# An LSTM and a GRU over one sequence on one core: the input weights are split by tick 1, and the LSTM's third step stands ahead of the condition's products and of the GRU's first step

## The reference

```
x (32, 128, 512), cond (32, 512)
# 1: LSTM over 128 steps, h0 = cond, c0 = 0
a  = x_t @ Wx + b + h @ Wh           # 2048 columns: i, f, o, g
c  = sigmoid(f)*c + sigmoid(i)*tanh(g);   h = sigmoid(o)*tanh(c)
x  = x + hs                          # y in the kernel
# 2: GRU over 128 steps of y, h0 = 0, with a condition
z  = sigmoid(y_t @ W_z + h @ U_z + cond @ C_z + b_z)
r  = sigmoid(y_t @ W_r + h @ U_r + cond @ C_r + b_r)
hh = tanh(y_t @ W + (r*h) @ U + cond @ C + b)
h  = (1-z)*h + z*hh
return y + hs
```

## Time and profile before

| | us |
|---|---|
| median of three executions | 1199.74 |
| the profiled execution's own time | 1200.66 |
| its span, first to last instruction | 1198.9 |
| TensorE busy | 1176.5 (98%) |
| VectorE busy | 981.0 (82%) |
| ScalarE busy | 464.0 (39%) |
| GpSimd busy | 334.0 (28%) |
| mean granted TensorE clock | 0.997 |

### The profile page before, as it was taken

How to read it: one execution, slowest core, us unless ns; L and a number is a source line. 1 busy time by engine, 2 the same in 40 slices (tenths; PEclk the granted TensorE clock), 3 DMA queues, 4 the chain that set the end, 5 groups by cost and what they waited for, 6 DMA issues and landing times.

```text
span 1198.9 us, 75562 instructions
## 1 busy us (share of the span) xinstructions
PE 1176.5 (98%) x34514; PEld 863.3 (72%) x34514; DVE 981.0 (82%) x2906; ACT 464.0 (39%) x1117; POOL 334.0 (28%) x614
## 2 busy tenths in 40 slices
PE   7899999999999999999999999999999999999997
PEld 2477676666667777777787777877777777777775
DVE  3869777888878888888888888888888888888876
ACT  5664334344333333333333333333333333333332
POOL 0100233333222223233232232322223323223221
PEclk9999999999999999999999999999999999999999
DMA  9701401111011111011111001111101111101001
GB/s 377 259 4 22 154 11 21 21 21 21 5 21 21 22 22 21 6 22 22 22 22 22 13 13 22 22 22 22 18 9 22 22 22 22 22 7 19 13 13 21
DMA packets 138272, 43.73 MB, mean 36 GB/s; under 512 B 131504, under 2 KB 131520, under 8 KB 136416
## 3 DMA queue, kind: packets, MB, share of 16 engines
q1 hardware_dynamic: 137632, 38.55, 13.2%
q10 hardware_dynamic: 192, 0.33, 0.1%
q0 software_dynamic: 128, 0.01, 0.0%
HBM read 30.49 MB, written 8.39 MB: 32 GB/s over the span
## 4 chain that ended last, share of the span: by engine, by line
PE 96%; DVE 2%; DMA 1%; issue 1%; ACT 0%; POOL 0%; SPq 0%; DVEq 0%; POOLq 0%
PE ps_g L996 40%; PE ps_l L996 34%; PE ps_l L1059 15%; PE ps_g L1005 3%; PE ps_c L1059 2%; PE ps_l L1005 2%; DMA stage<-in_L_cond_b_dram 1%; DMA wh<-in_L_cond_Wx_dram 1%; DVE wh L671 0%; DVE zr L674 0%; DVE rg L916 0%; ACT zr L584 0%; DVE rgT L918 0%; DVE wx L671 0%; DVE rg2T L668 0%
## 5 line engine op out<-in xcount | busy, mean ns | idle before, releaser
L996 PE MATMUL ps_l<-wh,h2T 128*32 128x512 f16 x5952 | 345.1, 380 | 0.3 <-issue 0.3
L996 PE MATMUL ps_g<-w,y2T 128*32 128x384 f16 x5760 | 256.3, 326 | 0.0
L996 PEld LDWEIGHTS ps_l<-wh,h2T 128*32 128x32 f16 x5952 | 157.1, 97 | 132.8 <-issue 1.9
L996 PEld LDWEIGHTS ps_g<-w,y2T 128*32 128x32 f16 x5760 | 159.3, 97 | 87.6
L429 POOL TENSOR_TENSOR yT<-xT,hT 128x128 f32<-128x128 f32 x128 | 61.9, 483 | 531.0 <-DVE hT L853 531.0
L996 PE MATMUL ps_g<-u,g2T 128*32 128x256 f16 x5760 | 179.5, 273 | 0.0
L996 PEld LDWEIGHTS ps_g<-u,g2T 128*32 128x32 f16 x5760 | 156.2, 97 | 14.6
L674 DVE SCALAR_TENSOR_TENSOR zr<-ps_g,sc,term 128x256 f32<-128x256 f32 x128 | 61.8, 483 | 76.9 <-PE ps_g L996 74.6
L382 POOL TENSOR_TENSOR o_area<-yT,gT 128x128 f32<-128x128 f32 x127 | 58.2, 458 | 192.2 <-DVE gT L977 191.4
L996 PE MATMUL ps_g<-u,rg2T 128*32 128x128 f16 x5760 | 102.7, 219 | 3.1 <-DVE rg2T L668 2.9
L612 ACT ACTIVATE g2T<-gT,sc 128x128 f16<-128x128 f32 x120 | 48.3, 402 | 131.6 <-DVE gT L977 131.6
(11 more groups left out here) (140 smaller groups left out, 1799.2 us busy)
## 6 DMA issues: line engine op xcount, KB each, us to landing
out_dram<-o_area SPq DMA_DIRECT2D x124, 64.0 KB, 1.9
x_nat<-in_x_dram SPq DMA_DIRECT2D x120, 64.0 KB, 2.7
wh<-in_L_cond_Wx_dram SPq DMA_DIRECT2D x4, 1024.0 KB, 8.8
stage<-in_L_cond_Wx_dram SPq DMA_DIRECT2D x4, 1024.0 KB, 9.9
w<-in_L_cond_Wh_dram SPq DMA_DIRECT2D x3, 1024.0 KB, 15.6
u<-in_L_cond_Wh_dram SPq DMA_DIRECT2D x1, 1024.0 KB, 21.0
stage<-in_L_cond_W_z_dram SPq DMA_DIRECT2D x1, 1024.0 KB, 23.2
stage<-in_L_cond_W_r_dram SPq DMA_DIRECT2D x1, 1024.0 KB, 25.5
```

Of the source, the lines that this page charges most:

```text
L996: mm = nc.tensor.matmul(bank[B * j:B * j + B, c0:c1].rearrange("p (n c) -> p n c", c=B), still(a, k), moving(b, k, j), start=opens and (a, ...
```

## The change

The GRU's biases get a slab of their own and are loaded at the start, and spread at chunk 3 of `wx`. The input's products of step 2 go from the loop over `wx` into tick 0, between the chunks of h0 with `wh`, and those of step 3 stand half there and half behind. All of `wx` is split by the end of tick 0: on ScalarE `wx_high(3)` before tick 0, on VectorE `wx_low(2)` before it and `wx_low(3)` behind its state. The LSTM's step 2 (`T_AHEAD`) moves on every engine from tick 2 into tick 1: on TensorE behind y(0) with W and ahead of the condition's products, on VectorE into the row of `wh_low`, ahead of the condition's sum and of the GRU's step 0. All four `wh_high` stand ahead of it on ScalarE.

```diff
+        T_AHEAD = T_WH + 1
-        biases = stage[0:1, GG + 2, :]
+        l_biases, g_biases = stage[0:1, GG + 1, :], stage[0:1, GG + 2, 0:GG * D]
@@ gpsimd
-            pool.wait_ge(spread_ps, 1)
             for g, b in enumerate((b_z, b_r, b_h)):
...
@@ scalar
             wx_high(2)
+            wx_high(3)
             wh_squared(1)
...
                 if t == T_WH:
-                    wx_high(3)
...
                     wh_high(2)
+                    wh_high(3)
...
             def after_cand(t):
-                if t == T_WH:
-                    wh_high(3)
...
-                if runs_lstm(t):
...
+                if runs_lstm(t) and t != T_AHEAD:
+                    lstm_step(t)
...
                 if t == T_WH:
                     after_state(t)
+                    lstm_step(T_AHEAD)
@@ vector, before tick 0
+            dve.wait_ge(spread_ps, 2)
+            nc.vector.tensor_copy(term1[:], ps_g[0][:, 0:GG * P]).then_inc(term_done, 1)
+            dve.wait_ge(term_done, 2)
...
             wx_low(1)
-            dve.wait_ge(spread_ps, 2)
-            nc.vector.tensor_copy(term1[:], ps_g[0][:, 0:GG * P]).then_inc(term_done, 1)
-            dve.wait_ge(term_done, 2)
+            dve.wait_ge(wx_hi, 2)
+            wx_low(2)
@@ vector, after_state
                 if t == 0:
-                    dve.wait_ge(wx_hi, 2)
-                    wx_low(2)
+                    dve.wait_ge(wx_hi, 3)
+                    wx_low(3)
                 if t == T_WH:
                     common(0, 0)
                     lstm_scales(1, 1)
-                    dve.wait_ge(wx_hi, 3)
-                    wx_low(3)
-
-                    wh_low(0, 0)
-                    wh_low(0, 1)
-                    wh_low(1, 0)
+                    for k in range(K - 2):
+                        for half in range(HALVES):
+                            wh_low(k, half)
+                    new_sums(T_AHEAD, T_AHEAD, 0)
+                    wh_low(2, 0)
+                    new_cell(T_AHEAD)
+                    wh_low(2, 1)
+                    new_state(T_AHEAD, T_AHEAD)
 
                     dve.wait_ge(cond_ps, 1)
...
             def after_keep(t):
                 if t == T_WH + 1:
-                    wh_low(2, 1)
+                    wh_low(3, 0)
...
             def after_cand(t):
-                if t == T_WH:
-                    wh_low(1, 1)
-                    wh_low(2, 0)
                 if t == T_WH + 1:
-                    wh_low(3, 0)
                     wh_low(3, 1)
@@ tensor
+                if k == 3:
+                    pe.wait_ge(bias1_in, 16 * GG)
+                    spread(ps_g[0], g_biases, GG * P)
+                input_as_given(0, k)
+                input_as_given(1, k)
...
+            def recurrent_as_given(t):
+                pe.wait_ge(hT_done if t > 0 else h0T_done, max(t, 1))
+                state = hT[:, (t - 1) % 2, :] if t > 0 else h0T[:]
+                for k in range(K):
+                    if t == 0:
+                        pe.wait_ge(wh_in[k], 16)
+                    done = as_given(ps_l[t], 0, state, wh_raw[k], k, False, k == K - 1)
+                    if t == 0 and k < 2:
+
+                        input_as_given(2, 2 * k)
+                        input_as_given(2, 2 * k + 1)
+                    if t == 0 and k == 2:
+                        input_as_given(3, 0)
+                        input_as_given(3, 1)
+                done.then_inc(gates_ps, 1)
+                if t == 0:
+                    input_as_given(3, 2)
+                    input_as_given(3, 3)
...
-                if t == 1:
+                if t == T_WH:
+
+                    recurrent_as_given(T_AHEAD)
 
                     pe.wait_ge(wh_scale, 1)
```

More of the change, by code:

```diff
@@ L566, in after_cand, with lstm_step @@
                     u_high(1)
+            def lstm_step(t):
+                act.wait_ge(tg_sum, t + 1)
+                nc.scalar.activation(tg_cell[:, 0:P], gates[:, 3 * P:4 * P], ACT.Tanh)
+                act.wait_ge(ifo_sum, t + 1)
+                nc.scalar.activation(ifo, ifo, ACT.Sigmoid).then_inc(ifo_done, 1)
+                act.wait_ge(cell_done, t + 2)
+                nc.scalar.activation(tanh_c[:], cell, ACT.Tanh).then_inc(tanh_c_done, 1)
             def tick(t, n, i):
@@ L845, in seventh_out, with new_sums, new_cell @@
                 evict(4, u, pre[:, (u + 1) % NL, H1], ps_l[(u + 1) % NL][:, H2], bias0(H1))
+            def new_sums(t, n, r):
+                dve.wait_ge(gates_ps, t + 1)
+                if t >= FW:
+                    dve.wait_ge(evicted, 2 * (t - FW) + 3 if t % 2 == 0 else 2 * (t - FW) + 2)
+                to_add = pre[:, t % NL, :] if t >= FW else term0[:].rearrange("p g c -> p (g c)")
+                undone(gates[:, 3 * P:4 * P], ps_l[t % NL][:, 3 * P:4 * P], r_l(r), to_add[:, 3 * P:4 * P]).then_inc(tg_sum, 1)
+                undone(ifo, ps_l[t % NL][:, 0:3 * P], r_l(r), to_add[:, 0:3 * P]).then_inc(ifo_sum, 1)
+            def new_cell(t):
+                dve.wait_ge(ifo_done, t + 1)
+                dve.wait_ge(cell_done, t + 1)
+                nc.vector.tensor_tensor(ig_fc[:], gates[:, 0:2 * P], tg_cell[:], ALU.mult).then_inc(ig_fc_done, 1)
+                dve.wait_ge(ig_fc_done, t + 1)
+                nc.vector.tensor_tensor(cell, ig_fc[:, 0:P], ig_fc[:, P:2 * P], ALU.add).then_inc(cell_done, 1)
             def new_state(t, n):
@@ L867, in tick @@
                 lstm, gru = runs_lstm(t), runs_gru(t)
-                if lstm:
+                if lstm and t != T_AHEAD:
                     if q == 0:
                         dve.wait_ge(scl_done, group + 1)
[L871 to L876, removed]
+                    new_sums(t, n, r)
                 if q == 0 and NG_W <= group + 1 < NG:
@@ L889, in tick @@
                 after_sums(t)
[L890 to L895, removed]
+                if lstm and t != T_AHEAD:
+                    new_cell(t)
                 after_cell(t)
@@ L909, in tick @@
                     undone(zr[:], ps_g[s % 2][:, 0:2 * P], r_g(r_s), term1[:, 0:2 * P]).then_inc(zr_sum, 1)
-                if lstm and t != T_WH:
+                if lstm and t not in (T_WH, T_AHEAD):
                     new_state(t, n)
@@ L1110, in _ @@
                     pe.wait_ge(bias0_in, 16)
-                    spread(ps_bound, GL * P)
-                for t in range(FL - 1):
-                    as_given(ps_l[t], 0, xT[:, 0, P * t:P * t + P], wx_raw[k], k, k == 0, False)
+                    spread(ps_bound, l_biases, GL * P)
+                if k == 3:
[3 more added lines that the diff above has]
+                input_as_given(1, k)
             pe.wait_ge(h0T_done, 1)
@@ L1129, in tick @@
                 if lstm and t < FL:
-                    pe.wait_ge(hT_done if t > 0 else h0T_done, max(t, 1))
-                    state = hT[:, (t - 1) % 2, :] if t > 0 else h0T[:]
-                    for k in range(K):
-                        if t == 0:
-                            pe.wait_ge(wh_in[k], 16)
-                        done = as_given(ps_l[t], 0, state, wh_raw[k], k, False, k == K - 1)
-                    done.then_inc(gates_ps, 1)
-                    if t == 0:
-                        for k in range(K):
-                            as_given(ps_l[FL - 1], 0, xT[:, 0, P * (FL - 1):P * FL], wx_raw[k], k, k == 0, False)
+                    if t != T_AHEAD:
+                        recurrent_as_given(t)
                 elif lstm:
```

18 lines of the change are left out of this document (6 added, 12 removed).

## The result

The changed kernel takes 1204.65 us, the median of sixteen executions (1199.24 to 1206.4), the kernel before 1199.97 beside it (1198.83 to 1202.68). The ratio is 1.0023, 95% interval 1.0014 to 1.0032. The prediction was 1200.3, range 1198.2 to 1202.4, most of the chance on no change that can be told: wrong, it is slower. The medians lie 0.39% apart, more than the ratio says; the executions fall into groups, so neither number is one thing.

A forecast was written before the change was run, and what follows sets the result against it. VectorE's list of work was taken to bound the kernel from step 1's sums to gT, which the time follows. That chain's -0.4 and the clock's +1.0 gave +0.6 on 1199.74: 1200.3 us, range 1198.2 to 1202.4.

The forecast's parts named there:

- TensorE's idle time bounds nothing but the head; the time follows gT's readers: Whole run: TensorE unbroken from 58.39 us, so time follows when gT of GRU step 0 is ready, before at 53.81.
- The head: Start up to step 1's sums: bias wait gone, VectorE sets step 0's sums at 28.55 against 30.45, 1.9 us earlier.
- The 0.19 us for a slow matmul: Head, first 24 matmuls in 4.64 us: 0.19 us each at the half clock, so 16 take chunk 0 to 10.7.
- VectorE's list: Step 1's sums to gT: VectorE's work is the bound, +1.5 us, from 16.37 to 17.9.
- the sum -0.4: At gT's readers: head and VectorE's work together bring them to 53.4 to 53.5 against 53.81, -0.4 us.
- The blocks of 128 matmuls: TensorE's "issue" gaps: blocks of 128 matmuls with loads; one arrives near 48.2 in y(1)'s products, two idle us off the chain.
- What the clock does: At gT: TensorE idles 3.2 us to 53.4; a fall to 1.2 GHz slows gT's 64 matmuls, 0 to +1.95 us.
- the term "+1.0": At gT's 64 matmuls: price taken for the clock's fall, half of +1.95 us, since it need not meet all.
- its nearest row: 24 matmuls in 4.48 us instead of 2.7, a factor of 1.65, giving 1.3 us for the fall at gT.
- "1.8 us; I take it as not enough": Gap before step 1's product, 30.0 to 31.8: 1.8 us idle, taken as too short for the clock to fall.
- rival 2: Clock falls twice, before step 1's product and at gT: +2.9 us, 1202.6 us; chance 0.13.

The follow-up runs named there:

- e1: Changed kernel with 32 thrown-away matmuls in tick 2, between y(1)'s products and the wait for gT; ratio 1.0011, median 1202.74 us.
- e13: Changed kernel with 16 thrown-away matmuls in tick 0's gap only, behind step 3's input products; ratio 1.001, median 1202.39 us.
- e5: Changed kernel with thrown-away matmuls in both gaps, 16 in tick 0 and 32 ahead of gT; ratio 1.0004, median 1201.82 us.
- e4: Kernel before with only LSTM step 2 ahead and its wh_high/wh_low order; biases, input products, wx split as before; ratio 1.0047, median 1205.79 us.
- e6: e2 with 16 thrown-away matmuls in tick 0's gap; ratio 0.998, median 1198.72 us.
- e9: Kernel before the change with 16 thrown-away matmuls in its wait for the GRU's biases; ratio 0.9999.
- e3: Changed kernel with LSTM step 3's product moved from the head of tick 3 to tick 2, ahead of the wait for gT; ratio 0.9991, median 1198.99 us.
- e2: Changed kernel without the step ahead: only early biases, input products in tick 0 and early wx split; ratio 0.9974, median 1197.68 us.
- e12: e2 with wh_low(2, 0) moved on VectorE from tick 1 to behind keep in tick 2; ratio 0.9976, median 1197.85 us.
- e10: e13 with 16 more thrown-away matmuls between gT's products and the wait for rgT in tick 2; ratio 1.0008, median 1201.96 us.

## Why the prediction was wrong

- **TensorE's idle time bounds nothing but the head; the time follows gT's readers.** Right: the earlier trace rows has them at 53.81, the changed kernel at 53.84, e1 at 53.80, and e1's span is within 0.2 us of the old one. Not to the tenth, though: e13's y(2) starts 0.25 us ahead of the kernel before's and its span is 1.0 us shorter, e5's gives away 0.8 us, both behind 62 us, where TensorE has the same work in the same order.
- **The head.** Right in its mechanism: no wait for the bias, VectorE and not TensorE sets step 0's sums. The shift was 1.35 us and not 1.9 (30.45 to 29.11): the first 16 matmuls took 3.64, not 3.04, and the chunk landed 0.2 later, so the squares came at 19.34, not 18.75. The 0.19 us for a slow matmul was the mean of a row in which 16 ran slowly and 8 fast; slow ones start four at a time every 0.85 us, 0.21 each, double the 0.11. The prediction calls them "at the half clock". Their pace is that of the rows with 0.50, but the profile's clock column has 1.00 there.
- **VectorE's list**, +1.5. Right: from 36.09 to 53.84 is 17.75, forecast 17.9. e4 hit its number to 0.05 us by the same terms. So the sum -0.4 should have been 0.0.
- **The blocks of 128 matmuls.** Right, and borne out by e5, e6 and e9: 16 matmuls more in front, and the gap moves 15 to 17 earlier. The time is a draw: the block in y(1)'s products came at 47.1, not 48.2, so the idle time there was 0.37 and the one ahead of gT 4.4 instead of 3.2; but in e1 and e3, whose TensorE does the same up to there, it came at 48.17 and 48.11. In e13's profile it comes at 48.0:

```profile
48.02 2.78 PE L1015 MATMUL ps_g<-stage,yT 128*32 128x128 f32 x90 [0.48 <-issue]
53.56 1.96 PE L1015 MATMUL ps_g<-stage,gT 128*32 128x128 f32 x64 [2.76 <-DVE gT L987]
```

There the gap is 2.76 and the clock holds.

- **What the clock does: the step that failed** is the term "+1.0", the price of the fall at gT. That the clock would fall there was right for the profiled execution. I let it slow only the 64 matmuls that read gT, +1.95 us at the most. In the profile it went on over rgT's idle time, its 32 matmuls and most of step 3's product, 10.2 us in all, and cost 3.4. With 0.0 for the rest the sum is 3.4 us, and the two profiled executions lie 3.5 apart. Why it went on so long is not shown: in e4, in the same chain behind 5.3 us of idle time, it lasted 3.4 us and cost 1.3, the very price that the prediction had worked out from its nearest row. All other falls traced before the tail (the kernel before, e2, e6, e9, e12, and e4's first) lasted 3.4 us too.
- The medians lie further apart than that, 4.7 us. The middles of the groups at 0.999 and 0.995 are 1200.1 and 1204.9; the 1.4 us that this is above the traced 3.4 is not explained.
- **"1.8 us; I take it as not enough"**, the first gap. It came out as 2.2 us, and behind 2.2 us the clock fell in the profiles of e2 and e12 and held in those of the changed kernel, e1 and e3. So it is no safe gap. But rival 2, both falls, at 0.13 and 2.9 us, is not what the profile shows: by the mean clock at most the three executions at 0.993 of sixteen can be it.
- Behind both: one profiled execution showed gaps of 1.7 to 2.2 us of which one brought a fall, and I read that as three safe gaps and an exception. It was one draw; a few other executions of the kernel before had more time at half clock (three of 26 and two of 33 at 0.993, 1202.28 to 1205.58 us).
- The Trainium skill ("TensorE: Matmul & The Clock Gate", "HAM oscillation") has the mechanism, idle gaps between bursts that send the clock back to half; the 52 to 62 us of the changed kernel agree.

What stays open: how long an idle time must be to make the clock fall here, why one fall lasts 3.4 and another 10.2 us, what makes e1's second group, and what makes the remaining 2 us of spread at a full clock (e5), most of which arises behind 62 us in the one trace compared.

## What to carry to other kernels

A step brought forward on a serial chain moves idle time together; count the longest gap that the new order gives the matrix engine, not only the sum. Where a gap exceeds those that the kernel has now, price the clock's fall over the chain behind it and not only over the next burst, as a range (here 1.3 us in one trace and 3.4 in another), and time enough executions to see the groups: the median of three may show only one. Do not count falls by the mean clock of a span; look where in the trace they are, and leave out the time behind the last matmul. Take a change apart before judging it: here one half is worth 0.26% and the other, alone, costs 0.47%.

## What was not expected of the hardware

- What is in all likelihood instruction fetch shows in matmul counts: idle times of 0.2 to 2.7 us at a distance of 128 matmuls with their weight loads. Those above 1.1 us all came while the large loads ran (DMA share 0.8 to 1.2), and 16 matmuls added ahead move them by 15 to 17.
- Thrown-away matmuls are not free even in idle time: they keep the clock where they stand and move such gaps, and in e6 and e9 the clock fell behind the moved gap instead.
- At a mean clock of 0.999 or more the same program spreads over 1.2 us (changed kernel) to 2.3 us (e5).
- Behind gaps of 2.2 us the clock fell in some executions and held in others; behind 2.8 us (e13, e10) it held in the one profiled; a fall lasted 3.4 us in seven cases and 10.2 in one.
- The clock also falls behind the last matmul, in every trace here, which lowers the mean and costs nothing.
